# Phase 5's residual: from a load and a VectorE addition per step to an adding transfer on GpSimd's queue

## What is computed

```
out_conv = conv1d(x, weight, groups=4, taps=9) + ctx + bias     # x: (32, 128, 2048) fp32
h   = out_conv regrouped as rows of 2048
ffn = h @ W + ffn_bias + (h @ A_eff^T + h @ A_shared^T) @ (B_eff, B_shared)^T   # W: (2048, 2048)
out = x + ffn                                                   # x is added once to every output
```

## Time and profile before

| | |
|---|---|
| median of three runs | 1656.8 us (1656.36 to 1657.97) |
| the profiled execution, own time | 1654.82 us |
| its span in the trace | 1653.0 us |
| busy: TensorE matmul / VectorE / ScalarE / GpSimd | 1641.2 / 1220.0 / 737.5 / 156.0 us |
| DMA traffic | 434.97 MB, mean 263 GB/s |
| DMA queues: SyncE's q1 / GpSimd's q0 | 353.69 MB, 63.9% / 75.51 MB, 17.1% of 16 engines' span |

### The profile page before, as it was taken

The page is one execution under the profiler, slowest core; times in us unless marked ns, Lnnn a source line. Parts: engine busy times, 40 slices in busy tenths (PEclk is TensorE's granted clock), DMA queues, the critical chain, the costliest instruction groups (busy, mean ns, idle before and its releaser), DMA issues. The chain is left out here.

```text
span 1653.0 us, 22362 instructions
## 1 busy us (share of the span) xinstructions
PE 1641.2 (99%) x8240; PEld 1401.2 (85%) x8240; DVE 1220.0 (74%) x1777; ACT 737.5 (45%) x978; POOL 156.0 (9%) x200
## 2 busy tenths in 40 slices
PE   9999999999999999999999999999999999999999
PEld 6799888898888899999998888887888888888887
DVE  7888888984465689999996545459989645567776
ACT  7766776744222575566661312144444311223221
POOL 0001001110152000000000134000000000001000
PEclk9999999999999999999999999999999999999999
DMA  8968777986887758877776798679999898998886
GB/s 249 282 225 289 259 247 257 318 279 183 288 308 269 239 187 295 288 253 242 255 261 216 254 322 309 235 226 250 268 268 244 293 328 316 315 317 259 230 230 172
DMA packets 192772, 434.97 MB, mean 263 GB/s; under 512 B 51956, under 2 KB 91476, under 8 KB 188024
## 3 DMA queue, kind: packets, MB, share of 16 engines
q1 hardware_dynamic: 170664, 353.69, 63.9%
q0 software_dynamic: 20992, 75.51, 17.1%
q10 hardware_dynamic: 1008, 4.34, 0.9%
HBM read 279.05 MB, written 154.42 MB: 262 GB/s over the span
## 5 line engine op out<-in xcount | busy, mean ns | idle before, releaser
L2295 PE MATMUL acc<-w_hi,y_t 128*128 128x512 f32 x2560 | 710.5, 391 | 2.4 <-DVE w_lo L1505 1.1
L2295 PEld LDWEIGHTS acc<-w_hi,y_t 128*128 128x128 f32 x2560 | 474.3, 188 | 98.1 <-issue 2.1
L2295 PE MATMUL acc<-w_lo,y_t 128*128 128x512 f32 x1280 | 395.5, 390 | 0.0
L2295 PEld LDWEIGHTS acc<-w_lo,y_t 128*128 128x128 f32 x1280 | 240.4, 188 | 51.2
L1131 ACT COPY x_q<-x_raw 32x512 f32<-32x512 f32 x248 | 269.6, 1087 | 20.4 <-DVE x_lo L1606 13.4
L2160 PE MATMUL cps<-cw,x_hi 128*128 128x256 f32 (+2 forms) x1088 | 244.1, 313 | 0.4 <-DVE x_lo L1799 0.4
L2160 PE MATMUL cps<-cw,x_lo 128*128 128x384 f32 (+2 forms) x768 | 181.1, 283 | 0.0
L2160 PEld LDWEIGHTS cps<-cw,x_hi 128*128 128x128 f32 x1088 | 176.5, 189 | 3.6 <-DVE x_lo L1799 1.2
L1176 ACT CAST y_t<-g 128x1024 fp32r<-128x1024 f32 x63 | 66.4, 1054 | 194.6 <-PE acc L2295 154.3
L1599 DVE COPY x_q<-x_raw 32x512 f32<-32x512 f32 x248 | 147.8, 596 | 4.4
L2160 PEld LDWEIGHTS cps<-cw,x_lo 128*128 128x128 f32 x768 | 135.2, 188 | 0.0
(11 more groups left out here) (243 smaller groups left out, 2190.7 us busy)
## 6 DMA issues: line engine op xcount, KB each, us to landing
g<-U SPq DMA_DIRECT2D x80, 512.0 KB, 7.3
A<-g SPq DMA_DIRECT2D x64, 512.0 KB, 4.4
g<-A SPq DMA_DIRECT2D x64, 512.0 KB, 5.7
x_raw<-in_x SPq DMA_DIRECT2D x31, 1024.0 KB, 5.2
U<-g SPq DMA_DIRECT2D x48, 512.0 KB, 5.2
g<-in_L_ffn_kernel POOLq DMA_DIRECT2D x32, 512.0 KB, 6.2
T<-g POOLq DMA_DIRECT2D x32, 512.0 KB, 4.6
g<-in_x SPq DMA_DIRECT2D x32, 512.0 KB, 6.5
```

What stands on the lines that cost most here:

```text
L2295: ins = T.matmul(acc[:, b, m, :], y_buf[b][:, c, part, :], wt[:, w, m * 512:(m + 1) * 512], start=(c == 0 and part == 0 and wt is w_hi), s ...
```

## The change

In phase 5 the residual is no longer loaded into `xres` by SyncE and added by VectorE. Instead GpSimd issues, for each of the 16 steps, a transfer from `x` onto `stage[u % 2]` that adds to what is there. It waits for `stage_in` (the load of the sums has landed) and counts up `step_res`, for which `evac(u)` waits in place of `pre_added`. Phase 1 keeps its load and its addition. The waits for pair 12 and 13 of phase 6 no longer need a `pre_add`, since `xres` is unused in phase 5.

```
+        step_res = [sem("step_res0"), sem("step_res1")]
...
                 elif F == 4:
                     sp.wait_ge(s_out[0], 16 * NP)
                     sp.wait_ge(pre_added, NP)
                 else:
-                    sp.wait_ge(pre_added, 2 * NP + n - 13)
+                    sp.wait_ge(w_lo_ready, w_no(4, 13) + 1)
+                    sp.wait_ge(bias_ready, 2)
...
-                if f in LORA_PHASES and u != 5 * NP:
+                if f == 1:
                     load_xres(u)
...
-                    load_xres(5 * NP)
...
             for r in range(2 * QS):
+                if r == QS:
+                    for u in range(5 * NP, QU):
+                        pool.wait_ge(stage_in[u % 2], 16 * ((u - NP) // 2 + 1))
+                        V.dma_start(stage[u % 2], x[2 * (u % NP) + 1][:, HALF:L], accum_op=ALU.add).then_inc(step_res[u % 2], 16)
...
-                    dve.wait_ge(pre_added, lora_index(u) + 1)
+                    if u // NP == 1:
+                        dve.wait_ge(pre_added, lora_index(u) + 1)
+                    else:
+                        dve.wait_ge(step_res[b], 16 * (u % NP // 2 + 1))
...
-                    pre_add(pu)
+                    if pf == 1:
+                        pre_add(pu)
...
-            pre_add(QU - 1)
```

More of the change, by code:

```diff
@@ L422, in pair_stage @@
             return st[:, t_no(F, n) % 4] if n < 12 else xres[n % 2]
-        def xres_no(u):
-            return u % NP // 2 + (NP // 2 + 2 if u // NP == 5 else 1)
         def has_conv(u):
@@ L676, in load_xres @@
                     sp.wait_ge(pre_added, n - 1)
-                elif f == 1:
+                else:
                     sp.wait_ge(form_out, 64 * NCH)
[L679 to L686, removed]
+                sp.dma_start(xres[b], x[2 * p][:, 0:HALF]).then_inc(xres_in[b], 16)
             def load_b(u):
@@ L1077, in split_pair @@
                 else:
-                    act.wait_ge(xres_in[n % 2], 16 * (NP // 2 + 1 if F == 4 else NP + 2))
+                    act.wait_ge(xres_in[n % 2], 16 * (NP // 2 + (1 if F == 4 else 2)))
                 if n < 6:
@@ L1713, in pre_add @@
                 dve.wait_ge(stage_in[b], 16 * ((u - NP) // 2 + 1))
-                dve.wait_ge(xres_in[b], 16 * xres_no(u))
+                dve.wait_ge(xres_in[b], 16 * (n // 2 + 1))
                 V.tensor_tensor(stage[b], stage[b], xres[b], ALU.add).then_inc(pre_added, 1)
```

## The result

The changed kernel took 1658.78 us in the median of 20 runs (1656.64 to 1662.76), the kernel before 1656.21 us in 20 runs (1654.4 to 1657.97). The ratio is 1.0017, 95% interval 1.0011 to 1.0023: slower by about 2.8 us of 1656 (2.6 by the two medians). That is a real loss, and it lies within the 0.2% that the prediction called no change.

What follows compares the result with a forecast made beforehand. TensorE, 99% busy, was taken as the bound, with DMA just under its limit. Terms 0 + 0 + 1.4 + 2.8 gave +4.2 us: 1659.0 from the profiled 1654.8, 1661.0 us against the median 1656.8; range 1656.3 to 1669.

Steps and rivals of the forecast that it cites:

- VectorE's relief: Phases 5 and 6: removing 16 additions, 19.5 us in all, from half-idle VectorE was claimed to gain 0.
- The early end of the lead: Start of phase 6: time gained from VectorE's last addition ends as it idles 1.96 us before pair 11's split; gain 0.
- +1.27 us per step: Phase 5, DMA engines: an adding transfer of 2.78 us replaces a plain load of 1.51 us.
- The body: Phase 5's steps: fuller DMA engines and a longer `stage` chain were claimed to cost +1.4 us, with ends 0 and 11.
- overrun at the lora B load: Phase 5: backlog and slower transfers use up this load's 3.9 us of room, overrunning by 0 to 1 us.
- a microsecond in the `stage` chain: Phase 5: allowance for `evac` waiting on store, load of sums and an adding transfer of 8.0 us, which just fits.
- the 4.3 us: Phase 5: how late an `evac` may be before TensorE waits.
- rival C: Phase 5: the `stage` chain becomes the bound from 10 us per adding transfer; +11 us, 1668 us; chance 0.14.
- The step into phase 6: Last adding transfer in saturated DMA delays step 94's store, pair 11, VectorE's row, y load and TensorE: +2.8 us.
- The sum: Whole kernel: 0 + 0 + 1.4 + 2.8 = +4.2 us, forecast 1661.0 us.
- Rival B: Phase 5 and its end: queues absorb the transfers, so not slower; 1656.8, up to 1659 us; chance 0.34.
- What would show it: Profile signs: 2.8 us transfers, phase 5 DMA share at least 1.0, late `evac`, ScalarE's wait 2 to 3 us longer, TensorE idle.

Runs made afterwards that it cites:

- step 95 alone: Changed kernel with only step 95 using the adding transfer, steps 80 to 94 loading and adding as in the kernel before: ratio 1.0017 to the kernel before.
- pair 11 moved: Pair 11 issued ahead of phase 6's first pass_out load: changed kernel 1.0012, kernel before 0.9998, changed kernel with steps 93 to 95 put back 1.0003.
- thirteen kernels of the table: The kernel before, the changed kernel and the follow-up variants except double transfers, compared side by side in phase 6; ratios 0.9998 to 1.0017 to the kernel before.

## Why the prediction came out as it did

- **VectorE's relief is worth 0: right.** No residual at all gave 1.0003. The early end of the lead that was named, the wait before pair 11's split, is there after the change too, with 2.03 us.
- **The adding transfer costs 2.78 us of DMA time, the load 1.51, so +1.27 us per step: right for the first (2.80), too low for the load.** The 1.51 was the mean over all that q1 moved. When the loads went, q1 took 16.8% of 175 us less for 7.86 MB less, 1.96 us for each 0.524 MB (1.69 by the kernel without residual). So the net was 0.70 us per step by both queues' shares, about half of the forecast's. A plain transfer on GpSimd's queue at the same place measured 1.78, so the addition itself takes 1.0 us of the engines. The Trainium skill (DMA: Bandwidth & Descriptors, Anatomy of one DMA) gives one price for a transfer on GpSimd's path, by its size alone. From issue to landing adding and plain ones of one size took 8.3 and 6.9 us here, so the two traces disagree with one price for both, and the measurement decides.
- **The body, +1.4 us: the term that was mis-sized; it measured 0 in the profile.** Its two terms were an overrun at the lora B load, of which the middle of 0 to 1 us was taken, and a microsecond in the `stage` chain (0.5 and 1 are 1.5; the prediction writes 1.4). The first stood on a demand of 12.25 us per step against a capacity of 12.16; with the load at its real price the demand was 0.98 of 11.81, 11.6 us, below that capacity. The chain's lateness came to 2.1 us on VectorE in four places, 1.23 at most in one, inside the 4.3 us that the prediction had itself worked out as room. Having found the room, it should have charged nothing within it. Twice the transfers show where the room ends: one more step of 8 to 9 us in the chain costs 57 us. The mechanism of rival C is thus real, and the median of 8.3 us kept the changed kernel out of it; that it begins at 10 us per transfer wasn't run.
- **The step into phase 6, +2.8 us: near in size, right in its main links.** 2.04 us at pair 11's split, 2.51 at the y load, 2.57 at the last matmul. That one adding transfer at this place suffices was shown by step 95 alone (1.0017). Two links were different. The store of step 94 was issued 0.1 us late only, and pair 11 not late at all; it was in flight for 10.7 us in place of 8.2. And TensorE did not lose the time at one place behind the y load: three quarters of it were lost before that, at waits for VectorE's late row. Two things are not explained. Taking that one transfer away doesn't undo all (1.0009), nor does taking the last three (1.0008); only with pair 11 moved as well was it 1.0003. And that saturation is what stretches pair 11's flight is argued, not shown: from 5.6 us ahead of phase 6's first matmul to 18.4 behind it the DMA share was 0.99 to 1.04 in all thirteen kernels of the table, and no run has the last adding transfer outside such a stretch.
- **The sum.** +4.2 was forecast and 2.6 measured by the medians (2.8 by the ratio, interval 1.8 to 3.8); most of the 1.6 too much is the body's term. The other 0.6 us of the 2.2 us error is the starting point: the kernel before ran at 1656.21 beside the changed one, where the forecast had 1656.8.
- **Rival B, hidden,** is right for the body and wrong for the end. Its condition, an adding transfer that costs under 0.9 us more than the load, was met by the shares (0.70), and the time lies in its range. That the loss is real was only told by an interval much narrower than the 0.2% that was assumed. The forecast's range held all the same; that the body's term and the starting point were both too high moved the middle, not the range.
- **"What would show it":** transfers of 2.8 us, `evac` late in four steps, TensorE's later waits: there. The DMA share was to be at or above 1.0 in phase 5: it was 0.98, since the load's price was too low. ScalarE's wait for pair 11 was to grow by 2 to 3 us: it stayed at 2.29 us, since what stands ahead of it on ScalarE was late as well (the split of `b_raw`, after a wait of 4.55 us in place of 2.48). A wait's length was the wrong sign to name; the start of the instruction behind it was the right one.

## What to carry to other kernels

Taking work from an engine that is off the critical path gains nothing, and giving it to DMA engines that are near full can lose: count what a transfer takes of all engines, an adding one 1.6 times a plain one of the same size and queue here, and look at where it falls, not at the mean. The price of a plain load is better taken from what its queue's share loses without it (1.7 to 2.0 us here) than from the mean over all that the queue moves (1.5). A transfer that must wait for another one's landing runs late by that one's 8 us here; at the end of a phase this puts it into the next phase's first loads. And where a trace gives a room (4.3 us) larger than the lateness (1 us), charge nothing for it; spend the doubt on the place without room.

## What the runs showed of the hardware

- An adding transfer of 512 KB took 2.80 us of all 16 DMA engines, the same without the addition 1.78 (22.4% and 14.2% of 175 us, 14 transfers). GpSimd took 0.88 us to issue the one, 0.53 us the other; the medians from issue to landing were 8.3 and 6.9 us.
- The same y load of `one_pass(9)` took 8.6 to 11.5 us, and longest in the three kernels in which it was issued earliest, those with pair 11 moved (29.7 to 30.3 us after the first matmul: 10.8 to 11.5). Among the others it doesn't follow the time of issue: 8.6 us at 31.0, 10.1 at 31.9, 8.7 at 33.5. What it shares the engines with there wasn't taken apart.
- TensorE's clock, in the kernel with double transfers. Eight waits of 1.85 to 6.97 us each came with a stretch at 0.50 of full speed, TensorE's lower level of 1.2 GHz, of 3 to 10 us, and then the clock was back at its upper one. After the wait of 6.97 us that ended at 1364.34, and after the wait of 4.95 us at phase 6's first matmul:

```profile
1364.00:1371.00 7.00, 6.66 (x17) 5.24 (x18) 2.45 (x3) 0.75 (x1) 0.87 (x1) 0.54 0.88 271
...
1535.00:1541.00 6.00, 5.49 (x13) 4.36 (x14) 5.96 (x8) 2.09 (x3) 0.87 (x1) 0.50 0.61 172
1541.00:1548.00 7.00, 7.00 (x31) 5.64 (x31) 6.86 (x9) 3.10 (x4) 0.00 (x0) 0.99 1.05 321
```

TensorE made 13 matmuls from 1535 to 1541 and 31 from 1541 to 1548. In the changed kernel's phases 5 and 6 no wait was over 1.1 us, and the clock stayed at 1.00. (The columns are those of the first such fence.)
